# Pool takes the rotation's add, and the split into parts runs one turn behind

## What is computed

```python
h = _layernorm(x, ln1_g, ln1_b)
qkv = (h @ Wqkv).reshape(b, n, 3, H, dh)
q, k = _rotate(q, cos, sin), _rotate(k, cos, sin)   # r1 = x1*cos - x2*sin, r2 = x1*sin + x2*cos
s = einsum('bhqd,bhkd->bhqk', q, k) / sqrt(dh)      # causal mask, softmax, times v, @ Wo
```

## Time and profile before

| | us |
|---|---|
| median of 3 runs (1744.51 to 1754.33) | 1751.85 |
| the profiled execution's own time | 1748.37 |
| its span, first to last instruction | 1746.6 |
| busy: PE, DVE, ACT, POOL | 1456.7, 1251.3, 1169.6, 339.7 |

### The profile page before, as it was taken

One profiled execution on the slowest core, in us unless ns is written; L12 is line 12 of the kernel. 1 busy time (PEld: TensorE's weight loads), 2 busy tenths in 40 slices (PEclk: granted clock), 3 DMA queues, 4 the chain that ended last, 5 costly groups with the idle time before them and its releaser, 6 DMA issues.

```text
span 1746.6 us, 39193 instructions
## 1 busy us (share of the span) xinstructions
PE 1456.7 (83%) x15185; PEld 663.9 (38%) x15185; DVE 1251.3 (72%) x1974; ACT 1169.6 (67%) x2373; POOL 339.7 (19%) x386
## 2 busy tenths in 40 slices
PE   5579998989898888649999999899989979799840
PEld 3334444444443455402222222222222224789740
DVE  6787777878676257599999999799979952432333
ACT  7527777777777655408899998798878967334321
POOL 5310000000000156300000001100122341332435
PEclk9859999999899999958999999999999989899975
DMA  4512323223220335310011111002001311678751
GB/s 139 194 56 75 108 90 107 101 83 133 73 84 17 107 114 157 118 63 8 33 44 42 36 55 47 32 33 69 32 32 43 117 56 44 181 232 254 217 147 54
DMA packets 127770, 158.46 MB, mean 91 GB/s; under 512 B 14432, under 2 KB 100448, under 8 KB 127328
## 3 DMA queue, kind: packets, MB, share of 16 engines
q1 hardware_dynamic: 118368, 130.77, 24.0%
q0 software_dynamic: 9216, 25.18, 4.0%
HBM read 90.90 MB, written 68.96 MB: 92 GB/s over the span
## 4 chain that ended last, share of the span: by engine, by line
PE 23%; DVE 16%; DMA 9%; issue 9%; ACT 4%; POOL 3%; SPq 1%; ACTq 0%; POOLq 0%; DVEq 0%
DVE row_max L632 14%; DMA sorted_in<-v_all,slots 6%; PE bank L599 6%; PE banks L1423 4%; PE banks L1433 4%; PE banks L575 4%; PE banks L543 2%; ACT probs L686 2%; POOL probs L1253 2%; DMA qk_parts<-parts 2%; PE banks L1414 0%; PE banks L330 0%; ACT front L1981 0%; PE banks L1378 0%; ACT o_sums L697 0%
## 5 line engine op out<-in xcount | busy, mean ns | idle before, releaser
L632 DVE TENSOR_REDUCE row_max<-banks 128x2 f32<-128x1024 f32 (+3 forms) x896 | 939.3, 1101 | 139.2 <-PE banks L549 76.8
L686 ACT ACTIVATE probs<-banks 128x512 f32<-128x512 f32 (+3 forms) x1792 | 879.7, 551 | 194.8 <-PE banks L575 90.8
L599 PE MATMUL bank<-probs,v_ones 128*32 128x256 f32 (+3 forms) x7168 | 538.8, 378 | 19.8 <-ACT o_sums L697 16.8
L543 PE MATMUL banks<-k_work,q_work 48*128 48x512 bf16 (+3 forms) x1792 | 368.2, 383 | 75.9 <-DVE row_max L632 56.4
L575 PE MATMUL banks<-q_work,k_work 51*128 51x512 bf16 (+3 forms) x1792 | 386.9, 374 | 43.9 <-DMA q_work<-max_T 26.5
L575 PEld LDWEIGHTS banks<-q_work,k_work 51*128 51x128 bf16 x1792 | 102.8, 93 | 414.6 <-ACT probs L686 323.0
L599 PEld LDWEIGHTS bank<-probs,v_ones 128*32 128x32 f32 x7168 | 147.8, 109 | 259.9 <-ACT probs L686 187.6
L724 POOL DMA_DIRECT2D heads_out<-o_sums x64 | 35.6, 556 | 1015.7 <-ACT o_sums L697 1015.7
L1998 ACT ACTIVATE rope<-banks,expert 128x256 f32<-128x256 f32 x184 | 72.0, 474 | 121.5 <-PE banks L1423 121.5
L543 PEld LDWEIGHTS banks<-k_work,q_work 48*128 48x128 bf16 x1792 | 95.4, 96 | 140.1 <-DVE row_max L632 105.7
L1423 PE MATMUL banks<-rope,expert 128*128 128x256 f32 x368 | 95.7, 407 | 18.3 <-issue 12.1
(11 more groups left out here) (194 smaller groups left out, 1100.5 us busy)
## 6 DMA issues: line engine op xcount, KB each, us to landing
expert<-expert_rows SPq DMA_DIRECT2D x46, 578.0 KB, 4.7
qk_parts<-parts SPq DMA_DIRECT2D x64, 256.0 KB, 3.7
heads_out<-o_sums POOLq DMA_DIRECT2D x64, 256.0 KB, 4.4
sorted_in<-front SPq DMA_DIRECT2D x21, 512.0 KB, 7.2
q_work<-qk_parts SPq DMA_DIRECT2D x64, 128.0 KB
k_work<-qk_parts SPq DMA_DIRECT2D x64, 128.0 KB
parts<-sorted_in SPq DMA_DIRECT2D x46, 128.0 KB, 4.2
q_work<-qk_parts SPq DMA_DIRECT2D x64, 64.0 KB
```

The source lines that it names most:

```text
L543: last = pe.matmul(to[:, par, 0:width], q[r:r + M0, pair, qt * P:(qt + 1) * P], k[r:r + M0, pair, kh * G:kh * G + width], start=True, stop ...
L599: last = pe.matmul(bank[7][32 * j:32 * j + 32, c0 + part * w:c0 + (part + 1) * w], v_ones[i % QB][:, kt, j, :], prob_slots[:, (e + j) % RI ...
L632: dve.tensor_reduce(row_max[:, qt, 2 * pair:2 * pair + 2, kh], self.buf_of("chunk", g, c)[:, :, 0:width], AX.X, ALU.max).then_inc(s["chunk ...
L686: act.activation(prob_slots[:, e % RING, 0:width], banks46[:, e % EXP_BANKS, 0:width], ACT.Exp, scale=SCALE).then_inc(s["exps"], 1)
```

## The change

Pool does the add of `rotate`, which has the same waits as before. VectorE does residual(n-1) behind rope(n), and ScalarE middle(n-1) ahead of high(n), so that residual, middle and low all lag one turn. SP stores the middle and low parts of turn n-1 behind the high part of turn n; the loads of the attention keep their place. What is left of turn 7 is done behind each loop. The new orders: VectorE rope(n), residual(n-1), moments(n+2). ScalarE keep(n), input(n+1), middle(n-1), high(n), z(n+2), ln(n+2). Pool rotate(n), low(n-1), root(n+2).

```diff
                     attend[1].load(sp, n - LOAD_FROM)
-                proj[1].store(sp, n, 1)
-                proj[1].store(sp, n, 2)
+                if n:
+                    proj[1].store(sp, n - 1, 1)
+                    proj[1].store(sp, n - 1, 2)
                 if n == 1:
                     for to, src in masks:
                         sp.dma_start(to, src).then_inc(loaded_masks, 16)
+            for part in (1, 2):
+                proj[1].store(sp, GROUPS - 1, part)
@@ Pool
             for n in range(GROUPS):
+                proj[1].rotate(pool, n)
                 if n:
                     proj[1].low(pool, n - 1)
@@ VectorE
                 proj[1].rope(dve, n, n % HALVES)
-                proj[1].rotate(dve, n)
+                if n:
+                    proj[1].residual(dve, n - 1)
                 if n + 2 < GROUPS:
                     first_moments(n + 2)
-                proj[1].residual(dve, n)
+            proj[1].residual(dve, GROUPS - 1)
             attend[1].dve(dve)
@@ ScalarE
                     proj[1].input(act, n + 1)
+                if n:
+                    proj[1].middle(act, n - 1)
                 proj[1].high(act, n)
-                proj[1].middle(act, n)
                 if n + 2 < GROUPS:
                     first_z(n + 2)
                     first_ln(n + 2)
+            proj[1].middle(act, GROUPS - 1)
```

More of the change, by code:

```diff
@@ L355, in rope, with rotate @@
                         dve.scalar_tensor_tensor(to, src, b_qk[:, i:i + 1], table, ALU.add, ALU.mult).then_inc(s["products"], 1)
-            def rotate(self, dve, n):
+            def rotate(self, eng, n):
                 s = self.s
-                dve.wait_ge(s["products"], 4 * n + 4)
+                eng.wait_ge(s["products"], 4 * n + 4)
                 if n:
-                    dve.wait_ge(s["rest"], n)
-                dve.tensor_tensor(rot[:, :, :], t_cos[:, :, :], t_sin[:, :, :], ALU.add).then_inc(s["rot"], 1)
+                    eng.wait_ge(s["rest"], n)
+                eng.tensor_tensor(rot[:, :, :], t_cos[:, :, :], t_sin[:, :, :], ALU.add).then_inc(s["rot"], 1)
             def residual(self, dve, n):
```

## The result

The changed kernel took 1771.72 us (median of 4 runs, 1766.61 to 1779.26) against 1752.84 us for the kernel before in the same comparison: a ratio of 1.0128, 95% interval 1.0081 to 1.0176. It is slower, and clear of no change. The profiled execution took 1771.66 us with a span of 1769.8 us, 23.2 us over the 1746.6 us of before. All medians and ratios here are of undisturbed executions; two of the ten of the run with both edits at once, 2525.97 and 3027.5 us, were in another state and are left out.

The account below looks back on a forecast made before the run. The first stage was taken as bound by its engines in turns 0 to 5, by SP's DMA queue in 6 and 7. 1748.4 + 24.0 = 1772.4 us, or 1775.8 from the median; forecast 1774, range 1760 to 1783.

Parts of the forecast that it names:

- Pool's add, 2.4 us from the f32 row: Rotation's 128x1024 f32 add on Pool: 2.1 to 2.5 us, taken as 2.4 from the row with the same output type.
- Pool's order sets the turn, 9.5 us from the start of keep to the next: First stage: Pool's low(n-1) waits for middle, root(n+2) queues behind low, z waits for root; 9.5 us a turn against 8.1.
- high(5) 6.1 us late: ScalarE, turn 5: after the longer turns high(5) ends at 68.4 us against 62.33.
- the lock: Shared port: VectorE's residual may hold Pool's small product by up to 1.1 us; three turns 3.3 us, taken as 0.
- at most 5.40: TensorE, turn 5: eight matmuls take at most 5.40 us, so rotation(5) does not hold high(5).
- The landing behind a load, 15.2 us after its first issue: SP's queue: a middle store behind an attention load lands 15.2 us after the load's first issue; store(4,1) 84.7, store(5,1) 103.1.
- the first rival: Late landings are backlog; stores land 2.9 us after issue, stage 10.3 us later, 1758.7 to 1762.2 us; 10%.
- low(6) holds residual(7), the first row maximum at 107.8: Stage's end: residual(7) needs high(7), 105.1, and low(6), 106.3; first row_max about 107.8 against 83.81, 24.0 us late.
- A shift of the stage's end is a shift of the whole: VectorE's first row_max at 83.81 us ends the stage; what moves it moves all behind, nothing makes the time up later.
- ScalarE's attention work stays hidden: Behind load(2), low(7) ends by 126.4 us; ScalarE needs its first transposed maxima at 133.0, leaving 6.6 us of cover.
- The second rival: VectorE was the bound and is relieved; stage up to 9.6 us earlier, 1738.8 to 1742.3 us; 4%.
- The third: The lock takes its price and landings take 16.8 us; 6.5 us more, 1778.9 to 1782.3 us; 16%.

Follow-up runs that it names:

- the run with both edits at once: Changed kernel with the lagging stores ahead of SP's loads and root ahead of low on Pool; ratio to before 1.0026, first row maximum at 88.20 us.
- the stores ahead: Changed kernel with SP's loads of the attention moved behind the two lagging stores of their turn; ratio to before 1.0055.
- one load: Changed kernel with load(0) at its place in turn 5, load(1) and load(2) behind the loop's last stores; ratio to before 1.0092, first row maximum at 94.41 us.
- all three comparisons: Changed kernel with root and stores ahead against kernel before: loads uncut (1.0026), both with loads in halves (1.0030 against 0.9990), both with load(0) in quarters (0.9995 against 1.0004).

## Why the prediction came out

The forecast was 1774.0 us and slower; measured 1771.72. In the profile, step by step:

- *Pool's add, 2.4 us from the f32 row*: 2.35. Its nearest row of the right output type served; the bf16 row of the same size would have given 2.1.
- *Pool's order sets the turn, 9.5 us from the start of keep to the next*: 9.4 in three turns of five, and z waits for Pool's product in each. Root ahead of low gave turns of 7.5 to 8.7, so the mechanism is shown.
- *high(5) 6.1 us late*: it ended at 69.46 against 62.33, 7.1 late. The missing 1.0 us is in the two turns of 10.0, each with its own reason. In the first the lock took its price: the product took 0.84 and not 0.20 us (the fence above), started at 33.52 beside a residual of 33.08 to 34.30. I had bounded that with 1.1 us a turn and taken 0; it came to 0.64 in one turn of five. In the second, TensorE's slow products of turn 3 brought the add on Pool late, to 47.33, and low(2) behind it; this I had not priced. The eight matmuls took 6.54 us there at a granted clock of 0.56 of full speed, so mostly at the lower of its two levels, behind 2.76 us in which TensorE had waited for z and 2.03 more for hT, where those of turn 2 took 3.70 us at 1.00. The "at most 5.40" of the prediction was wrong even of the kernel before, whose turn 0 took 5.76, but the rotation that it bounded did not hold high(5).

```profile
38.78 6.54 PE L330 MATMUL banks<-hT,w_qk 128*128 128x512 f32 x8 [2.03 <-ACT hT L393]
```

- *The landing behind a load, 15.2 us after its first issue*: 14.2 behind load(0) (70.54 to 84.69), 13.7 behind load(1) (87.72 to 101.44). middle(5) was forecast at 84.7 and middle(6) at 103.1. That middle(5) came out so close is luck: high(5) was 1.0 us later and the landing 1.0 us shorter than forecast. Both landings were shorter than forecast by 2.5 us together, which is the grain of truth in the first rival, where it claimed 14. Four runs bear it out for load(1): it went out 17.2 us behind load(0) here and 12.0 us before, where the landing took 16.8; with high ahead of middle it went out 10.7 us behind load(0), and the landing took 17.0 (85.38 to 102.37); with root ahead of low it was 17.6 us behind, and the landing took 13.6 (83.64 to 97.24). Less the 1.0 us above, the 2.5 us make 1.5 of the 1.7 us by which the sum was too long.
- *low(6) holds residual(7), the first row maximum at 107.8*: 106.14, released by low(6). That it is low and not high was in the sum (106.3 against 105.1), and the run with high ahead shows it.
- *A shift of the stage's end is a shift of the whole*: 22.3 became 23.2 us of span. That these two lie so close is luck, since single executions scatter by some 9 us; by the medians the change cost 18.9 us (14 to 31), and the forecast of 24.0 us was 5 too long, within that interval. With 1774 against 1771.72 it looks better than it was, as it started from 1750 and the median before was 1752.84. The runs agree within their scatter: 8.8 us with the stores ahead gave 0.55%, which is 9.6 us; 10.6 with one load gave 0.92%, 16 us (interval 10 to 22).
- *ScalarE's attention work stays hidden*: middle(7) started at 118.05, and the first transposed maxima at 131.34 (forecast 133.0) were released by TensorE, not by low(7).

The second rival, VectorE relieved, found nothing: with the lag, moving the add off or on VectorE did not move the stage's end by more than 0.1 us, though there landings hold the end and could hide a gain. The better test is root ahead of low with the add on Pool, where low no longer delays root: its turns are no shorter on average than the 8.0 us of before. The third, the lock and landings of 16.8 us, paid 0.64 of its 3.3 us, and the landings went the other way. What the prediction missed altogether lay outside its sum, and came out only in the experiments: that the add without the lag would cost 9 us.

Open: with both costs away the stage still ends 4.4 us late (88.20 against 83.81), with middle(6) waiting to 83.50 for a landing behind load(0); that rest was not taken apart further. A kernel with the lag, both edits and the add back on VectorE was not run, so it is open whether the lag or the add makes the 3.3 to 4.4 us that stay in all three comparisons (88.20 against 83.81, 90.63 against 86.67, 85.77 against 82.44). And what stretches the landing behind a load was inferred from the busy share of the DMA engines and from its price per load (10.8 us); a load spread over more engines was not tried.

## What to carry to other kernels

When a step is put off by one turn, list every wait that now falls into the same turn as its consumer, and every queue in which it changed places: here low got ahead of root on Pool, and a store got behind a load on SP, and these two made 4 and 13.5 of 22 us, while the moved arithmetic, in the kernel as changed, made none. A transfer whose completion frees a buffer should be issued ahead of bulk loads whose data nobody needs yet. Where a step waits for two others, moving up the one that is queued visibly first may free nothing: look up which one released it.

## What the runs showed of the hardware

VectorE's moments ended with three operations on 128x4 elements. Beside Pool's add of two SBUF tensors the first of them took 1.29 us where it took 0.17 in the kernel before (at 29.98 us). The last took 2.10 us beside `low` in the kernel with only the add on Pool (the fence there), where it took 0.16 alone. The statistics of 128x128 elements just before the first ran at their usual 0.86 us under the same add. VectorE's time line of the changed kernel, where Pool's add runs from 26.93 to 29.28:

```profile
26.71 0.86 DVE L1481 BATCH_NORM_STATS2 stats<-probs 128x6 f32<-128x128 f32 x4
27.61 0.38 DVE L1485 BATCH_NORM_AGGREGATE mv<-stats 128x2 f32<-128x6 f32 x4
28.02 1.29 DVE L1491 TENSOR_SCALAR first_var<-mv 128x4 f32<-128x4 f32 x1
```

So an operation of 16 bytes a row can stand still for as long as the other engine's large one. The Trainium skill (SBUF — State Buffer, SBUF: two separate sides) names VectorE's two-port modes as well as two SBUF inputs among what takes the shared pair. These rows, with one tensor input, agree with it if the operations ran in such a mode, which no row shows.
